# Reordering a graph network's attention tail: column sums earlier, head rows later, products of zeros before the transposes

## The reference

```python
h = relu(layernorm(x))
# layer 0: one logit per edge, softmax over edges with the same dst
feat  = concat([h[src], h[dst]])              # edges 0..255, 256..1535, 1536..8191
e     = relu(feat @ W_kind + b_kind)          # three kinds: hh, oo, ho
logit = e @ W_a + b_a
alpha = exp(logit - max_dst) / sum_dst(exp(...))
z     = segment_sum(alpha * h[src], dst)
x     = x + relu(concat([h, z]) @ W_node + b_node)   # rows 0..127 W_hn, the rest W_on
# layer 1: normalised adjacency with self loops
h     = relu(layernorm(x))
out   = x + sum_edges(deg^-.5[row] * deg^-.5[col] * (h[col] @ W + b))
```

## Time and profile before

| | |
|---|---|
| median of 3 runs | 582.92 us (582.46 to 585.1) |
| profiled execution, its time | 580.54 us |
| its span | 578.7 us |
| mean granted TensorE clock | 0.965 of full |
| TensorE busy | 526.1 us (91%) |
| VectorE busy | 418.4 us (72%) |
| ScalarE busy | 273.3 us (47%) |
| GpSimd busy | 193.1 us (33%) |

### The profile page before, as it was taken

The page is one execution under the profiler, slowest core; times in us unless marked ns, Lnnn a source line. Parts: engine busy times, 40 slices in busy tenths (PEclk is TensorE's granted clock), DMA queues, the critical chain, the costliest instruction groups (busy, mean ns, idle before and its releaser), DMA issues.

```text
span 578.7 us, 7213 instructions
## 1 busy us (share of the span) xinstructions
PE 526.1 (91%) x2136; PEld 365.5 (63%) x2137; DVE 418.4 (72%) x883; ACT 273.3 (47%) x432; POOL 193.1 (33%) x177
## 2 busy tenths in 40 slices
PE   0799989999998799888999799986989999999997
PEld 0688757777775467643444357742457878878885
DVE  6756336874659799779888797799596379888262
ACT  1723431211223898945644662999265274244200
POOL 3290030007466565526555654772301000000000
PEclk9999989999999799998999988998976999999999
DMA  8899385449999999999999999999891476304021
GB/s 309 322 330 383 123 281 183 146 142 246 392 344 341 344 347 289 346 312 329 372 341 355 361 338 362 312 279 216 284 371 50 169 236 197 114 2 132 14 91 54
DMA packets 55838, 146.95 MB, mean 254 GB/s; under 512 B 6770, under 2 KB 6898, under 8 KB 55410
## 3 DMA queue, kind: packets, MB, share of 16 engines
q0 software_dynamic: 22352, 81.28, 45.0%
q1 hardware_dynamic: 27936, 54.54, 26.4%
q10 hardware_dynamic: 5506, 10.56, 5.0%
HBM read 127.47 MB, written 18.87 MB: 253 GB/s over the span
## 4 chain that ended last, share of the span: by engine, by line
PE 57%; DVE 13%; DMA 12%; ACT 10%; issue 4%; POOL 2%; ACTq 1%; DVEq 0%
PE ps L844 34%; DMA gath<-tab_a,tabl_i 6%; PE ps L794 6%; ACT onehot L640 4%; PE ps L1037 4%; PE ps L1090 4%; PE ps L1068 3%; DVE ring_l L1182 2%; ACT late_onehots L640 2%; DMA gath<-tab_b,tabl_i 2%; DMA raw<-in_L_gnn_W_hn_dram 2%; PE ps L974 2%; PE ps L1003 1%; DVE gath L1207 1%; DMA raw<-in_L_gnn_W_on_dram 1%
## 5 line engine op out<-in xcount | busy, mean ns | idle before, releaser
L844 PE MATMUL ps<-ring_h,actT_h 128*128 128x512 f32 x376 | 160.9, 428 | 6.7 <-DVE actT_l L1177 3.1
L844 PE MATMUL ps<-ring_h,actT_l 128*128 128x512 f32 x376 | 149.2, 397 | 0.0
L844 PE MATMUL ps<-ring_l,actT_h 128*128 128x512 f32 x376 | 149.0, 396 | 0.0
L640 ACT ACTIVATE onehot<-onehot,lgs 128x512 bf16<-128x512 bf16 x156 | 100.0, 711 | 45.3 <-DVE onehot L1250 44.6
L580 ACT CAST ring_h<-raw 128x512 fp32r<-128x512 f32 x128 | 76.1, 622 | 93.6 <-PE ps L844 66.0
L1182 DVE TENSOR_TENSOR ring_l<-raw,ring_h 128x512 fp32r<-128x512 f32 x128 | 85.5, 687 | 44.6 <-ACT ring_h L580 36.3
L402 POOL DMA_INDIRECT gath<-tab_a,tabl_i x62 | 68.8, 1109 | 95.9 <-DVE gath L1207 46.2
L416 POOL DMA_INDIRECT gath<-tab_b,tabl_i x36 | 65.0, 1807 | 89.9 <-DMA tab_b<-stage 45.2
L844 PEld LDWEIGHTS ps<-ring_h,actT_h 128*128 128x128 f32 x376 | 72.1, 192 | 29.6 <-DVE actT_l L1177 3.3
L1207 DVE SCALAR_TENSOR_TENSOR gath<-gath,wa_b 128x1024 f32<-128x1024 f32 x62 | 75.9, 1226 | 20.2 <-DMA gath<-tab_b,tabl_i 19.2
L844 PEld LDWEIGHTS ps<-ring_h,actT_l 128*128 128x128 f32 x376 | 72.0, 191 | 15.8
(11 more groups left out here) (206 smaller groups left out, 702.3 us busy)
## 6 DMA issues: line engine op xcount, KB each, us to landing
raw<-in_L_gnn_W_ho_dram SPq DMA_DIRECT2D x32, 256.0 KB, 6.9
raw<-in_L_gnn_W_oo_dram SPq DMA_DIRECT2D x32, 256.0 KB, 5.8
raw<-in_L_gnn_W_hh_dram SPq DMA_DIRECT2D x32, 256.0 KB, 8.4
raw<-in_L_gnn_W_on_dram SPq DMA_DIRECT2D x32, 256.0 KB, 6.7
raw<-in_L_gnn_W_hn_dram SPq DMA_DIRECT2D x32, 256.0 KB, 7.4
tab_a<-stage ACTq DMA_DIRECT2D x16, 256.0 KB, 8.2
tab_b<-stage ACTq DMA_DIRECT2D x16, 256.0 KB, 5.1
raw<-in_L_gnn_W_dram SPq DMA_DIRECT2D x16, 256.0 KB, 3.5
```

Of the source, the lines that this page charges most:

```text
L640: ins = nc.scalar.mul(place[:, 1 + i, :], place[:, 1, :], lgs[:, i, q:q + 1])
L844: mm = nc.tensor.matmul(ps[:, first + m, :], w, v, start=(k == 0 and i == 0), stop=(k == KT - 1 and i == 2))
```

## The change

1. `close_banks` behind the last tile of each kind goes, and with it the semaphore; `copy_kind` waits for the semaphore that each tile's last matmul raises anyway.
2. `adj_columns` with `dinv` moves from behind `head_rows(1)` to step 7 of chunk 13, and writes to bank 4 in place of bank 1. The copy to `wrow` moves to VectorE's position (14, 2), and the opening of kind 2 at (14, 2) waits for it, as it reuses the bank.
3. `head_rows(0)`: k 0 to 3 behind the sums of (15, 1), k 4 to 7 behind all sums.
4. Ahead of each of the four row blocks' transposes, and ahead of the wait for its attention rows, stand six matmuls of zeros, 128x512 in bf16, into bank 0.

```diff
-        LAST_OF_KIND = (T_HO - 1, ET - 1, TG - 1)
+        LAST_OF_KIND = (T_HO - 1, TG - 1, ET - 1)
...
                     if q == TG:
-                        pe.wait_ge(s_degin, 1)
+                        pe.wait_ge(s_dinv, 2)
                         pe.wait_ge(s_copied, base + 6)
                         open_masked(2)
...
                     add_logits(q, q % TC)
-                    if q in LAST_OF_KIND:
-                        close_banks(s_kind, KIND_BANK[kind_of(q)])
...
+                    if (c, k) == (1, 7):
+                        pe.wait_ge(s_dinv, 1)
+                        pe.wait_ge(s_degin, 1)
+                        adj_columns(4, lambda k: dinv[:, k:k + 1])
...
             for c in (14, 15):
                 for k in range(KT):
+                    sums(c, k)
                     if (c, k) == (15, 1):
-                        head_rows(0, range(6))
-                    if (c, k) == (15, 2):
-                        head_rows(0, range(6, KT))
-                    sums(c, k)
+                        head_rows(0, range(4))
+            head_rows(0, range(4, KT))
             head_rows(1, range(KT))
-            pe.wait_ge(s_dinv, 1)
-            adj_columns(1, lambda k: dinv[:, k:k + 1])
             q = nth_split(CH_EDGE + 2)
             pe.wait_ge(s_kfree, 3 * NM)
             for m in range(NM):
+                for _ in range(6):
+                    nc.tensor.matmul(ps[:, 0, :], zeros_r[:, 0:P], zeros_r[:, :], start=True, stop=True)
                 pe.wait_ge(s_att, m + 1)
...
             for f in range(KT):
-                if f == 1:
-                    pe.wait_ge(s_dinv, 2)
...
-                dve.wait_ge(s_kind, (2, 3, 1)[t])
+                dve.wait_ge(s_ohu, OS + ET + ORDER[LAST_OF_KIND[t]] + 1)
...
+                    if (q, k) == (14, 2):
+                        dve.wait_ge(s_deg, 2)
+                        nc.vector.tensor_copy(wrow[:, :], ps[:, 4, 0:NM]).then_inc(s_dinv, 1)
...
-            dve.wait_ge(s_deg, 2)
-            nc.vector.tensor_copy(wrow[:, :], ps[:, 1, 0:NM]).then_inc(s_dinv, 1)
```

More of the change, by code:

```diff
@@ L208, in gnn_kernel @@
         s_seed = sem("inverse_seeds")
-        s_kind = sem("kind_counted")
         s_kfree = sem("kind_banks_free")
@@ L813, in open_masked, with close_banks @@
                     nc.tensor.matmul(ps[:, KIND_BANK[t] + b, :], ident_b[:, :], mask_b[t][:, b, :], start=True, stop=False, skip_group_check=True)
-            def close_banks(done, first=0):
-                for b in range(first, first + NM):
+            def close_banks(done):
+                for b in range(NM):
                     mm = nc.tensor.matmul(ps[:, b, :], zeros_r[:, 0:P], zeros_r[:, :], start=False, stop=True, skip_group_check=True)
```

## The result

The changed kernel is slower: 585.71 us median (582.58 to 589.14, 12 runs) against 582.36 (578.36 to 586.48, 12 runs), ratio 1.0086 with a 95% interval of 1.0058 to 1.0115, that is about 5.0 us; the two medians are 3.35 us apart. Forecast were 582.5 us and no change. The median lies in the range, the direction doesn't.

A forecast was written before the change was run, and what follows sets the result against it. Bound: TensorE's tail behind the head-weight transfer, with the softmax ending nearly together. Column sums save 7 us; late loads cost about 3, zeros 6.3, the clock returns 2.3: 0.4 sooner, 582.5 us, range 579.0 to 587.6.

The forecast's parts named there:

- The end of chunk 13 goes from 381.64 to 385.7, by 4.1; bounds 3.5 (no fall) and 5.3 (all nine slow).: Moved column sums at step 7: 3.5 us plus 0.6 for three of nine following matmuls at half clock, delaying ScalarE 3.9.
- Head row 7 then ends 1.6 later as before.: After the last head-weight load, taken to land at 428.8, the last head row ends at 430.4.
- The bound of 431.3: Latest landing of the last head-weight load, if it waits its 11.74 us again; 428.8 was taken, earliest 425.8.
- The zeros: 9.2 us for the blocks.: Four blocks of zeros and transposes before z, on the path: 3.4, 2.3, 1.75, 1.75 us; bounds 7.0 and 13.8.
- With the half clock comes a return.: Products for z begin at full clock after the zeros: the 96 take 22.0 us in place of 24.25, returning 2.3.
- the forecast's own 580.2 to 585.4: The forecast's own range for the whole kernel's time, without the rivals; chance 0.50.
- half clock through all blocks: Rival at zeros and transposes: clock stays at half, blocks take 13.8 us, +4 us, about 586.9; chance 0.17.
- rival 2: Last head-weight load lands before 427 and the clock is up: -3.9 us, about 579; chance 0.17.
- rival 3: Half clock at tiles 58 to 61 delays the last load's issue to 424, landing at 432: +3 us, about 586; chance 0.12.
- rival 4: Moved column sums are hidden, the end of chunk 13 doesn't hold ScalarE: some 3 us sooner, 579.5; chance 0.04.

The follow-up runs named there:

- after_again: The changed kernel, unaltered, measured and traced a second time: 584.52 us against 581.38 for the kernel before, ratio 1.0043.
- a_no_zeros: The changed kernel without its 24 products of zeros: 580.12 us against 580.77 for the kernel before, ratio 0.9972.
- b_no_close: The kernel before with only the closes taken away: 580.50 us against 580.37 for the kernel before, ratio 0.9975.
- n_behind: The changed kernel without zeros and with the column sums behind the end of chunk 13: 578.90 us against 580.22 for the kernel before.
- b_heads: The kernel before with only the head rows moved to the new order: 581.48 us against 580.37 for the kernel before, ratio 1.0013.
- b_cols: The kernel before with only the column sums moved to step 7 of chunk 13: 587.35 us against 581.38, ratio 1.0118.
- n_behind_heads: The changed kernel without zeros, column sums behind chunk 13, head rows in their old order: 579.14 us against 580.22 for the kernel before.
- n_behind_reload: n_behind with the reload of h held back until eight head rows are done: 580.57 us against 580.22 for the kernel before.
- a_cols_back: The changed kernel with column sums and wrow copy put back behind the head rows: 586.18 us against 580.77 for the kernel before, ratio 1.0113.
- b_zeros: The kernel before with only the 24 products of zeros added: 583.64 us against 580.37 for the kernel before, ratio 0.9987.
- n_behind_reload_zeros: n_behind_reload with the 24 products of zeros: 580.94 us against 580.22 for the kernel before, ratio 1.0006.
- a_cols_behind_heads_back: The changed kernel, zeros kept, with column sums behind chunk 13 and head rows in old order: 577.66 us against 581.38 for the kernel before, ratio 0.9963.
- a_cols_behind: The changed kernel with the column sums nine matmuls later, behind the end of chunk 13: 583.62 us against 580.77 for the kernel before, ratio 1.0050.
- a_late_reload: The changed kernel with the reload of h held back until fifteen head rows are done: 584.54 us against 580.37 for the kernel before, ratio 1.0062.

## Why the prediction was wrong

The mechanism of each part was right: the sums hold the end of chunk 13 and through it ScalarE, VectorE and the reload of h; the loads set the head rows; all zeros are on the path. Four terms were off. z starts at 96.7 and not 90.9 (95.6 in after_again):

1. **"The end of chunk 13 goes from 381.64 to 385.7, by 4.1; bounds 3.5 (no fall) and 5.3 (all nine slow)."** This is the step that failed first. I let the clock fall 1.5 us behind the sums, as in the one place that the trace showed, and the worst case let it fall at their end. It fell inside them: 6.3 us, and the sums themselves slow down. In six of the seven traces with the sums at that place ScalarE's copy waits 5.8 to 6.4 us; in a_no_zeros, whose clock held, it waits 3.3. One fall seen once is a draw, not a size: even in chunk 12, at the place that the trace showed, the clock fell behind the sums in fifteen of eighteen traces, inside them in two and not at all in one. Price here: +2.1, to the reload of h.
2. **"Head row 7 then ends 1.6 later as before."** In the kernel before one head row is left when the last transfer lands. In the changed one the last transfer waited for was the fifth load's, and four rows were left behind it, partly at half clock: 5.4 us in place of 1.6, +3.8. The landing itself is 20.5 us behind the reload and not 18.6: +1.9. The bound of 431.3 was for the landing alone, 81.5 from the mark, and the landing at 82.9 passes that too. Why it is 1.9 later against the reload no run tells.
3. **The zeros: 9.2 us for the blocks.** They took 7.1 (440.90 to 447.99), as the clock was back before they began. From the last head row to the first product for z it is 8.3 us where I had 10.3: -2.0.
4. **"With the half clock comes a return."** The 2.3 us came (22.1 for the 96), but a_no_zeros has them too (22.0), and so has b_no_close (22.1), whose column sums are still in the tail. So they aren't the zeros' return here, and the zeros cost 5.2 for nothing. What brings the clock back is not settled: with no zeros it was up at the first product for z in these two and in n_behind, and down in the kernel before, b_heads, b_cols, n_behind_heads and n_behind_reload.

2.1 + 1.9 + 3.8 - 2.0 = 5.8 us, which is what z starts late against the forecast in this trace. The median is 3.2 us over the forecast, as the profiled execution is the slowest of its kernel. That the median lies in the range is owed to the range's reach for the rivals: it is over the forecast's own 580.2 to 585.4, and those bounds aren't the sum's either, which gives 579.5 to 585.0 (-3.4 to +2.1 on 582.92). That the sum was made along one chain hid the most useful fact: two chains end together there, the softmax and the loads with the head rows. b_cols shows it from one side (TensorE relieved, the softmax later: +6.0), a_cols_back from the other (the softmax 8 us sooner, TensorE burdened: no gain). Whether the parts add up the runs don't tell. Alone they are +6.0, +3.3, +1.1 and +0.1 in the medians (sums, zeros, head rows, closes), together +3.1 and +3.4; by the ratios they are +1.2, -0.1, +0.1 and -0.3%, which is the changed kernel's +0.9% within the intervals. In the traces z ends 6.1, 4.2, 3.9 and -2.2 us later, together 5.5 and 4.3, which speaks against adding.

Of the rivals, half clock through all blocks (the rule on transposes in the Trainium skill, "TensorE: Matmul & The Clock Gate", Part 4) did not come: the clock was up through all four blocks, and in b_zeros it rose in the second although transposes lay between. It even rose with nothing but transposes since a head row (b_cols, 0.50 at 438 to 439 us and 1.00 at 440 to 441) or since the column sums (b_no_close), while in the kernel before it stayed at half through sums and transposes. An early landing (rival 2) didn't come: it needed 77.2 us from the mark, and it was 82.9. Cold last sums (rival 3) came in part: the clock was at half from 412 to 416 us. Hidden sums (rival 4) are refuted by ScalarE's 6.04 us.

## What to carry to other kernels

Work moved from a tail into a stage whose bound is another engine isn't free if that engine waits for what comes behind it. The same sums nine matmuls later didn't hold ScalarE at all, but VectorE's row maxima still came 2.2 us later, and what the place is worth in the whole stayed within the spread of the runs. Filler for TensorE's clock belongs in front of a wait that is really waited: read in the trace whether the instruction behind it waits, and whether the clock is down there at all after the other edits. Even there no run shows a gain: zeros in waits cost nothing (n_behind_reload_zeros), and in a_cols_behind_heads_back the clock fell again behind them. Where a transfer sets the end, count what is still to be done behind it, not only when it lands.

## What the runs showed of the hardware

- Behind 32 back-to-back records of matmuls of one column (3.5 us at full clock) the clock falls, though TensorE is busy throughout: in 31 of the 33 streams that began at full clock over the eighteen traces. In 19 it fell at their end or up to 1.5 us behind them; in 12 it fell inside them (six of the seven in step 7 of chunk 13, 4.4 to 4.9 us each) and stayed down about twice as long, so that the nine dense matmuls that followed took 4.06 us in place of 2.05. What in these sums takes it down no run isolates.
- The clock can come back among transposes: in b_cols and b_no_close it rose with no other kind of matmul between the last head row or column sum and the rise; in the kernel before and in b_heads it did not.
- Loads of 256 KB from one queue land 11 to 13 us after issue when another queue was given 4 MB earlier (390 to 410 GB/s in all), some 2.0 us apart; without these no head row waits for one (a_late_reload).
- A start of the stage that no edit touches moved between 349.0 and 354.5 us over the profiled executions, more than the effect under study. The tail had to be read from a mark in the same trace.
